# A two-layer graph network on one core: the low output products move one step back, and the second layer norm moves to GpSimd

## The reference

```
u = layernorm(x + (adj @ x) @ W0 + b0)
qkv = u @ w_qkv                          # 8 heads of 64
attn = softmax(where(adj == 0, -inf, q k^T / 8))
o = (attn @ v) @ w_proj + b_proj
y = layernorm(u + o + layernorm(o) * gamma + beta)
```

## Time and profile before

| | |
|---|---|
| median of 3 runs | 3403.73 us (3402.18 to 3408.43) |
| the profiled execution | 3408.55 us, its span 3406.7 us |
| PE busy | 3326.9 us (98%), PEld 2761.2 (81%) |
| DVE, ACT, POOL busy | 2683.6 (79%), 2211.3 (65%), 1831.5 us (54%) |
| granted TensorE clock, mean | 0.989 |

### The profile page before, as it was taken

The page is one execution under the profiler, slowest core; times in us unless marked ns, Lnnn a source line. Parts: engine busy times, 40 slices in busy tenths (PEclk is TensorE's granted clock), DMA queues, the critical chain, the costliest instruction groups (busy, mean ns, idle before and its releaser), DMA issues.

```text
span 3406.7 us, 87775 instructions
## 1 busy us (share of the span) xinstructions
PE 3326.9 (98%) x31760; PEld 2761.2 (81%) x31760; DVE 2683.6 (79%) x6557; ACT 2211.3 (65%) x4629; POOL 1831.5 (54%) x2559
## 2 busy tenths in 40 slices
PE   7999999998999999999999999999999999999995
PEld 6888888886888888888888888888888888888884
DVE  7666666665788888888888888888888888888886
ACT  4444444434677777777777777777777777777774
POOL 4555555542355555555555555555555555555555
PEclk9999999998999999999999999999999999999997
DMA  5565565562111111111221111111111111122110
GB/s 188 170 197 176 172 194 179 172 189 80 29 54 51 54 51 51 51 51 56 68 67 52 51 51 51 54 51 53 51 51 53 51 51 51 51 67 67 57 38 35
DMA packets 345168, 279.61 MB, mean 82 GB/s; under 512 B 13664, under 2 KB 275808, under 8 KB 344928
## 3 DMA queue, kind: packets, MB, share of 16 engines
q1 hardware_dynamic: 344928, 275.83, 26.6%
...
## 4 chain that ended last, share of the span: by engine, by line
PE 65%; issue 15%; DVE 10%; POOL 9%; ACT 0%; SPq 0%; POOLq 0%; DMA 0%; DVEq 0%
PE bank L849 34%; PE bank L840 14%; PE bank L800 8%; PE bank L816 6%; POOL xb L302 5%; DVE ot L1149 4%; POOL ub L296 4%; DVE pt_lo L1131 3%; DVE probs L1114 2%; PE bank L851 1%; DVE inv_sums L1123 1%; DVE bias_row L1114 0%; PE bank L339 0%; POOL rstd L307 0%; DMA x_lo<-ut_lo 0%
## 5 line engine op out<-in xcount | busy, mean ns | idle before, releaser
L1020 ACT ACTIVATE pt_hi<-bank 128x512 fp32r<-128x512 f32 x1024 | 556.9, 596 | 663.8 <-PE bank L816 648.8
L1013 ACT ACTIVATE probs<-probs,bias_row 128x512 f32<-128x512 f32 x1024 | 733.9, 725 | 16.9 <-DVE bias_row L1114 8.3
L731 POOL TENSOR_SCALAR probs<-probs,inv_sums 128x480 f32<-128x480 f32 (+1 forms) x1024 | 688.9, 686 | 0.0
L1114 DVE CUSTOM_DVE_ANT_0 probs<-bank,mask_bias 128x512 f32<-128x512 f32 x1024 | 661.5, 684 | 8.3 <-PE bank L800 4.1
L1131 DVE TENSOR_TENSOR pt_lo<-bank,pt_hi 128x512 fp32r<-128x512 f32 x1024 | 657.4, 684 | 2.0 <-ACT pt_hi L1020 2.0
L728 POOL TENSOR_TENSOR probs<-probs,inv_sums 128x32 f32<-128x32 f32 x512 | 123.7, 242 | 832.5 <-DVE inv_sums L1123 832.5
L849 PE MATMUL bank<-x_hi,w_hi 64*128 64x512 f32 x1024 | 413.0, 403 | 13.4 <-DMA x_lo<-ut_lo 5.7
L851 PE MATMUL bank<-x_hi,w_hi 64*128 64x512 f32 x1024 | 413.2, 403 | 0.0
L849 PE MATMUL bank<-x_lo,w_hi 64*128 64x512 f32 x1024 | 409.9, 400 | 0.0
L851 PE MATMUL bank<-x_lo,w_hi 64*128 64x512 f32 x1024 | 409.7, 400 | 0.0
L816 PEld LDWEIGHTS bank<-ident,probs 64*128 64x128 f32 x8192 | 338.8, 139 | 74.1 <-POOL probs L731 6.7
...
## 6 DMA issues: line engine op xcount, KB each, us to landing
...
ut_hi<-ut_hi_sb SPq DMA_DIRECT2D x128, 256.0 KB, 4.1
ut_lo<-ut_lo_sb SPq DMA_DIRECT2D x128, 256.0 KB, 3.8
x_hi<-ut_hi SPq DMA_DIRECT2D x128, 256.0 KB, 4.4
x_lo<-ut_lo SPq DMA_DIRECT2D x128, 256.0 KB, 4.7
out_dram<-o SPq DMA_DIRECT2D x128, 256.0 KB, 3.2
ub_row<-u_beta_rows SPq DMA_DIRECT2D x124, 256.0 KB, 2.7
```

The source lines that it names most:

```text
L731: pool.tensor_scalar(probs[:, k % 2, a, cols], probs[:, k % 2, a, cols], inv_sums[:, k % 4, a:a + 1], 0.0, ALU.mult, ALU.add)\
L1013: act.activation(probs[:, k % 2, a, :], probs[:, k % 2, a, :], ACT.Exp, bias=bias_row[:, k % 4, a:a + 1], scale=-1.0, accum_out=sums[:, k ...
L1020: act.activation(turned_into(pt_hi, k, i), turned(i), ACT.Copy).then_inc(pthi_made, 1)
L1114: dve.tensor_tensor_reduce(probs[:, k % 2, a, :], s_bank[a][:], mask_bias[:, k % T, :], -SCALE, 3.0e38, ALU.add, ALU.min, bias_row[:, k % ...
```

## The change

The order of TensorE's work. In a group's last step only the pt_hi products are left. The pt_lo products (`low_outputs`) now come right behind the transposes of the next group's first step. The fills are spread anew: pairs 0 to 7 in the last step of the group before, 8 to 15, 16 to 35 and 36 to 47 in steps 0, 1 and 2. In steps 2 and 3 the scores come last, and the wait for the next transposes stands ahead of their last pair.

VectorE's pt_lo of a group's first step waits for the low products of the pair before, because they read the pt_lo of that pair while they run. The two halves are summed behind that, in the same step as before.

GpSimd now makes z and the result of the layer norms with one `tensor_scalar` each ((row - mean) * rstd), adds o to the loaded row in place, and makes ot_lo. VectorE keeps the statistics; its shifts go, except in the last batch's end. ScalarE's `scaled` and `result` go, except there. ScalarE's exponentials stand ahead of its other work in each step. The tables of steps are new, with R_STEP for the result; the next row block of u + beta is loaded once the last sum has been made.

```diff
+last_y_made = sem("last_y_made")
-O_STEP = [5, 7, 7, 11]
-Z_STEP = [7, 9, 11, 13]
-S_STEP = [9, 11, 13, 15]
-EARLY = (4, 6, 2)
-FILL = ((8, 4), (12, 4), (8, 0))
-BEFORE = [sum(EARLY) + sum(map(sum, FILL[:n])) for n in range(T - 1)]
+O_STEP = [7, 7, 8, 9]
+Z_STEP = [8, 10, 12, 14]
+S_STEP = [11, 12, 15, 16]
+R_STEP = [12, 16, 16, 17]
...
 def finish(b, last=False):
-            sp.wait_ge(ub_added, b * 4 + (n - 3))
+            sp.wait_ge(u_added, b * 4 + (n - 3))
-        sp.wait_ge(y_made, b * 4 + (n - 3))
+        if last:
+            sp.wait_ge(last_y_made, n + 1)
+        else:
+            sp.wait_ge(y_made, b * 4 + (n - 3))
...
 def scale(b, n):
+    pool.wait_ge(u_loaded, b * 64 + 16 * (n - 3))
+    pool.wait_ge(rstd_made[0], b * 4 + (n - 3))
+    pool.tensor_tensor(ub[:], o[:, n, :], ub[:], ALU.add)
+    pool.tensor_scalar(o[:, n, :], o[:, n, :], mean_var[:, n, 0, 0:1], rstd[:, n, 0:1],
+                       ALU.subtract, ALU.mult).then_inc(z_made, 1)
+def add_z(b, n):
-    pool.tensor_tensor(t[:], t[:], gamma_row[:], ALU.mult).then_inc(gamma_done, 1)
-def add_z(b, n):
-    pool.wait_ge(u_loaded, b * 64 + 16 * (n - 3))
-    pool.tensor_tensor(o[:, n, :], o[:, n, :], ub[:], ALU.add).then_inc(ub_added, 1)
+    pool.tensor_tensor(o[:, n, :], o[:, n, :], gamma_row[:], ALU.mult).then_inc(gamma_done, 1)
-    pool.wait_ge(ub_added, b * 4 + (n - 3))
-    pool.tensor_tensor(o[:, n, :], o[:, n, :], t[:], ALU.add).then_inc(u_added, 1)
+    pool.tensor_tensor(o[:, n, :], o[:, n, :], ub[:], ALU.add).then_inc(u_added, 1)
+def result(n):
+    pool.tensor_scalar(o[:, n, :], o[:, n, :], mean_var[:, n, 1, 0:1], rstd[:, n, 1:2],
+                       ALU.subtract, ALU.mult).then_inc(y_made, 1)
+def ot_lo_part(b, p):
+    pool.wait_ge(othi_made, b * 4 + (p + 1))
+    pool.tensor_tensor(ot_lo[:, p, :], ot[:], f32(ot_hi[:, p, :]), ALU.subtract)\
+        .then_inc(otlo_made, 1)
 def batch(b, last_part=True, more=True):
     for k in range(STEPS):
+        group, part = divmod(k, T)
+        results = rows_done(b, k, R_STEP, last_part)
+            for of_batch, n in results:
+                pool.wait_ge(rstd_made[1], of_batch * 4 + (n - 3))
-        for batch_row in rows_done(b, k, 1, last_part):
-            power(*batch_row, 1)
+        for _, n in results:
+            result(n)
+        if part == 3 and group == 1:
+            ot_lo_part(b, 0)
+            power(b, n, 0)
-        for n in rows_at(k, O_STEP) if last_part else ():
-            power(b, n, 0)
+        for batch_row in rows_done(b, k + 1, R_STEP, last_part):
+            power(*batch_row, 1)
+        if part == 1 and group != 1 and (last_part or group > 0):
+            ot_lo_part(*pair_before(b, group))
...
+        if i == 2 and turn_next is not None:
+            ready_to_turn(*turn_next)
...
-        if end and m == T - 1:
-            if p < PAIRS - 1:
-                ready_to_turn(b, 4 * p + 4)
-            elif not (isinstance(b, int) and b == B - 1):
-                ready_to_turn(b + 1, 0)
...
-    def step(k, group, part):
-        filled = group == 0 or (last_part if group == 1 else more)
-        begin, (front, back) = BEFORE[part], FILL[part]
+    def filled(group):
+        return group == 0 or (last_part if group == 1 else more)
+    def fill_and_wait(group, first, count, k):
+        if filled(group):
+            fill(group, first, count - 1)
+        if k < STEPS or more:
+            ready_to_turn(b + k // STEPS, k % STEPS)
+        if filled(group):
+            fill(group, first + count - 1, 1)
+    def scores_ahead(k, turn_next=False):
+        if k + 3 < STEPS or more:
+            scores(b, k + 3, (b + (k + 1) // STEPS, (k + 1) % STEPS) if turn_next else None)
+        elif turn_next and k + 1 < STEPS:
+            ready_to_turn(b, k + 1)
+    def low_outputs(b, p, between=None):
+        attend_v(b, p, pt_lo, 1)
+        if between is not None:
+            fill(*between)
+        attend_v(b, p, pt_lo, 0)
+    def first_step(k, group):
-        fill(group, begin, front)
-        if k + 3 < STEPS or more:
-            scores(b, k + 3)
-        if part == 2:
-            group, begin, front, back = group + 1, 0, 0, EARLY[0]
-            filled = group < PAIRS and (last_part if group == 1 else more) or group == PAIRS and more
-        if filled:
-            fill(group, begin + front, back - 1)
-        ready_to_turn(b, k + 1)
-        if filled:
-            fill(group, begin + front + back - 1, 1)
+        if group > 0 or last_part:
+            low_outputs(*pair_before(b, group), (group, 8, 2) if filled(group) else None)
+        elif filled(group):
+            fill(group, 8, 2)
+        if filled(group):
+            fill(group, 10, 2)
+        scores_ahead(k)
+        fill_and_wait(group, 12, 4, k + 1)
+    def second_step(k, group):
+        turn(k)
+        if filled(group):
+            fill(group, 16, 10)
+        scores_ahead(k)
+        fill_and_wait(group, 26, 10, k + 1)
+    def third_step(k, group):
+        turn(k)
+        if filled(group):
+            fill(group, 36, 12)
+        scores_ahead(k, turn_next=True)
     def last_step(k, group):
-        fill(group + 1, EARLY[0], EARLY[1])
+        more_fill = filled(group + 1) and (group + 1 < PAIRS or more)
+        if more_fill:
+            fill(group + 1, 0, 6)
...
-        if k + 3 < STEPS or more:
-            scores(b, k + 3)
+        if more_fill:
+            fill(group + 1, 6, 2)
-        attend_v(b, group, pt_lo, 1)
-        fill(group + 1, EARLY[0] + EARLY[1], EARLY[2])
-        attend_v(b, group, pt_lo, 0)
+        scores_ahead(k, turn_next=True)
-        for part in range(T - 1):
-            step(T * group + part, group, part)
-        last_step(T * group + T - 1, group)
+        first_step(T * group, group)
+        second_step(T * group + 1, group)
+        third_step(T * group + 2, group)
+        last_step(T * group + 3, group)
+    if not more:
+        low_outputs(b, PAIRS - 1)
...
-def scaled(b, n):
-    act.wait_ge(shift_made[0], b * 4 + (n - 3))
-    if not (isinstance(b, int) and b == 1 and n == 0):
-        act.wait_ge(u_added, b * 4 + (n - 4))
-    act.activation(t[:], o[:, n, :], ACT.Identity, bias=shift[:, n, 0:1],
-                   scale=rstd[:, n, 0:1]).then_inc(z_made, 1)
-def result(b, n):
-    act.wait_ge(shift_made[1], b * 4 + (n - 3))
-    act.activation(o[:, n, :], rows_of(b, n)[0], ACT.Identity, bias=shift[:, n, 1:2],
-                   scale=rstd[:, n, 1:2]).then_inc(y_made, 1)
+def result(n):
+    act.wait_ge(shift_made, n + 1)
+    t_row = rows_of(B, n)[0]
+    act.activation(o[:, n, :], t_row, ACT.Identity, bias=shift[:, n:n + 1],
+                   scale=rstd[:, n, 1:2]).then_inc(last_y_made, 1)
 def unit_hi(b, k, i, more):
...
 def batch(b, last_part=True, more=True):
     for k in range(STEPS):
+        group, part = divmod(k, T)
+        if part == 3 and group == 1:
+            ot_hi_part(b, 0)
-        if output_at(b, k, 0) and (last_part or k >= T):
-            ot_halves(*output_at(b, k, 0))
-        if k % T == 1:
-            unit_hi(b, k, 0, more)
-            unit_hi(b, k, 1, more)
-        if k % T == 2:
-            unit_hi(b, k, 2, more)
-            unit_hi(b, k, 3, more)
-        if output_at(b, k, 1) and (last_part or k >= T):
-            ot_hi_part(*output_at(b, k, 1))
-        for n in rows_at(k, Z_STEP) if last_part else ():
-            scaled(b, n)
-        for batch_row in rows_done(b, k, 2, last_part):
-            result(*batch_row)
+        if part == 0 and (last_part or group > 0):
+            ot_halves(*pair_before(b, group))
+        if part == 1 and group != 1 and (last_part or group > 0):
+            ot_hi_part(*pair_before(b, group))
+        if part in (1, 2):
+            unit_hi(b, k, 2 * part - 2, more)
+            unit_hi(b, k, 2 * part - 1, more)
...
 def pt_lo_part(b, k):
+    if k % T == 0 and not (isinstance(b, int) and b * STEPS + k == 0):
+        dve.wait_ge(pv_done, b * 8 + k // 2)
...
-def ot_lo_part(b, p):
-    dve.wait_ge(othi_made, b * 4 + (p + 1))
-    dve.tensor_tensor(ot_lo[:, p, :], ot[:], f32(ot_hi[:, p, :]), ALU.subtract)\
+def last_ot_lo():
+    dve.wait_ge(othi_made, 4 * B)
+    dve.tensor_tensor(ot_lo[:, PAIRS - 1, :], ot[:], f32(ot_hi[:, PAIRS - 1, :]), ALU.subtract)\
 def statistics(b, n, i, rows_of):
...
+def rows_statistics(b, k, last_part):
+    for n in rows_at(k, O_STEP) if last_part else ():
+        first_statistics(b, n)
+    for batch_row in rows_done(b, k, S_STEP, last_part):
+        last_statistics(*batch_row)
 def batch(b, last_part=True, more=True):
     for k in range(STEPS):
...
+        if part == 0:
+            rows_statistics(b, k, last_part)
-        if output_at(b, k, 0) and (last_part or k >= T):
-            ot_sum(*output_at(b, k, 0))
-        for n in rows_at(k, Z_STEP) if last_part else ():
-            row_shift(b, n, 0)
-        if output_at(b, k, 2) and (last_part or k >= T):
-            ot_lo_part(*output_at(b, k, 2))
```

(42 more changed lines are left out.)

23 lines of the change are left out of this document (10 added, 13 removed).

## The result

The changed kernel took 3537.94 us (median of five runs) against 3406.73 us of the kernel before on the same chip: ratio 1.0383, interval 1.0371 to 1.0396; a sixth run took 4052 us with the granted clock at 0.75 instead of 0.988 and is not compared. The prediction said 3360 us and gave slower 11 in 100. The span of the profiled execution is 3533.6 us against 3406.7.

The account below looks back on a forecast made before the run. TensorE was taken as the bound, busy 80.01 of 80.31 us a batch. Terms -38.1 + 3 - 4 - 0.6 - 3.9 = -43.6 us gave 3360 us from a 3403.73 median; likeliest range 3347 to 3376, eight in ten 3345 to 3398.

Parts of the forecast that it names:

- the price of GpSimd's two row operations: GpSimd's z and result: 0.69 us for each tensor_scalar, taken from the probabilities' scaling.
- GpSimd's sum of 55 us: GpSimd's busy time per batch: 10.7 us more for z, result and ot_lo, 55 of 79 us.
- The queue argument: GpSimd, steps 12 to 15: the next probabilities' scaling queues behind leftover row work but is never late; least spare 1.0 us.
- The sign that it gave for B: TensorE's transposes waiting for GpSimd's probabilities in steps 15, 1 or 3, with a tensor_scalar over 1 us.
- Rival B: GpSimd becomes the bound through dearer row operations: 2.1 us a batch, 65 us, 3425 us; chance 0.10.
- TensorE's order: A group's 76 slots fall 19, 23, 15, 19; the halves-sum wait goes, gaining 1.27 us per batch, 38.1 in all.
- pt_lo's new wait: VectorE's pt_lo waits for the low products in first steps: 0.03 us stall a group, 3 us in all.
- rival A: pt_lo comes late in every first step: each 0.1 us costs 12.4, with 0.2 3385 us; chance 0.16.
- The ends: First and last batch: -4 for the first eight steps, -0.6 for batch 0's second half, -3.9 for the last batch.
- the 1.8: Last batch, step 8 to step 15's transposes: GpSimd's chain sets 31.5 us instead of 33.3.
- Nobody on the path waits for these.: ScalarE's scaling and result rows: removing them was claimed to touch no wait on the path; no gain was counted.

Follow-up runs that it names:

- spread_19: The minus-the-mean kernel with new step tables: no row statistics in a group's first step, row 3's result at step 19; 3368.92 us, ratio 0.9892.
- neg_mean: The changed kernel with z and the result as (o + minus the mean) * rstd, the negation made by VectorE; 3383.53 us, ratio 0.9927.
- mult_add: The changed kernel with z as o * rstd + mean and the result as u * rstd + 0.0, arithmetically wrong; 3382.11 us, ratio 0.9926.

## Why the prediction was wrong

**The step that failed** is the price of GpSimd's two row operations: "I take 0.69 for the tensor_scalar (it is the same instruction with other operands)", with bounds of 0.686 and 1.298. It measured 2.07. The row it was taken from multiplies and adds; the new one subtracts, and I looked at operand counts and not at the arithmetic. The two bounds came from rows of which neither held a subtract in a tensor_scalar, so neither was a bound. With multiply and add the price was right within 0.09 (0.77), and so was GpSimd's sum of 55 us.

**The queue argument was right, with the wrong number in it.** For step 13 the prediction has the scaling from 1.1 to 2.7 us after the transposes; it must end by 5.4 (5.84 less the 0.4 that its other limits allow). With the subtraction it ran from 5.2 to 6.7, and the step was 1.3 too long. With the addition (the kernel with minus the mean) it starts 1.37 after that step's transposes (2139.99) and costs nothing:

```profile
2141.36 0.26 POOL L687 TENSOR_TENSOR probs<-probs,inv_sums 128x32 f32<-128x32 f32 x1
```

Of the 3.8 us between the two, 2.6 are the longer result and z of step 12. The other 1.2 were there when step 12's scaling began (2.6 us into the step against 1.4): they came over from the steps before, and the prediction's working begins with step 13. The sign that it gave for B came true, transposes late at steps 15, 1 and 3 with a tensor_scalar over 1 us, but those at steps 14, 0 and 2 were late as well. Rival B was this mechanism, deciding "from 1.4 us a batch", at 2.1. Measured: 84.30 - 79.44 = 4.9 us a batch. It had 10 in 100, because its price ended at 1.30. The Trainium skill (GPSIMD Engine Reference, 4.1 Engine selection), on which B's chance was lowered, has elementwise add, mul and max with one input at roughly line rate on GpSimd. It names no subtract, so the prediction took more from it than it says. No row here has a tensor_scalar of this size on VectorE; its one-input statistics of 128x512 take 0.68 us, near the 694 ns of multiply and add, and not near the 2010 with subtract.

**TensorE's order: right.** Predicted steps 4.92, 5.84, 4.00 and 5.00; measured in the spread_19 kernel 4.93, 5.79, 4.02, 5.02, and 79.00 a batch against 79.1. The wait of TensorE's weights for the sum of the halves is in none of the lists of the kernels with the new order.

**pt_lo's new wait: mechanism right, size too small.** Taken 0.03 us for a group. With statistics ahead, the steps of the neg_mean kernel took 79.44 a batch where spread_19 took 79.00: 0.44 a batch against the 0.1 taken, some 13 us in all against 3. That is rival A at its price of 0.1 a first step (12.4 us). A part of it is the mend's own: the negation stands among the statistics, and step 8 took 5.16 us with it and 5.03 without it (mult_add). Without it the steps 0, 8 and 12 lose 0.16, 0.10 and 0.10, so 0.36 a batch.

**The ends: too large.** The first eight steps took 38.69 to 38.72 us against 39.84, a gain of 1.1, not 4 (the clock stood at 0.87 as before); the second eight gained 1.1 where 0.6 were predicted. From the last batch's start the end took 112.37 against 115.04, 2.7 of the 3.9 predicted, in spread_19. But not where it was predicted: from step 8 to step 15's transposes it took 33.31 us against 33.25 (3292.55 to 3325.86, 3331.66 to 3364.91), nothing of the 1.8, and 2.0 came behind these transposes, for which the prediction had no term. That so much of the 3.9 came is in part luck. The granted clock of the whole stretch was 0.85 against 0.81; what share of the gain is the clock's was not separated.

**ScalarE "loses the scaling and the result rows. Nobody on the path waits for these.": half right.** Nobody waited for them before. In the new order they would have cost 3415 - 3383 = 32 us in the place where I tried them, so moving them off is part of the gain and not a neutral item.

**The total.** With the subtraction gone and the tables mended, the same order ran in 3369 us against the 3360 forecast; of the 178 us between forecast and result, 155 are the subtraction (3538 to 3383), 14 the statistics' places (3383 to 3369) and 9 are left: some 4 are the ends, 2 come from the kernel before, which took 3405.57 us beside that run and 3403.73 beside the forecast, and 3 stay open.
